# Chunk states of an attention kernel: k turned by 32x32 blocks on VectorE and through memory, in place of TensorE's transposes

## The reference, cut to what matters

```python
k = _apply_rope((hidden_states @ Wk.T).reshape(B, L, KVH, D), cos, sin)
scores = jnp.einsum('bhnid,bhnjd->bhnij', qc, kc)
k_dec = kc * jnp.exp(Glast - G)[..., None]
cstates = jnp.einsum('bhnjd,bhnje->bhnde', k_dec, xc)
_, prev = lax.scan(step, init, (chunk_decay, cstates))   # state = state * dec + cs
y_inter = jnp.einsum('bhnid,bhnde->bhnie', qc * jnp.exp(G)[..., None], prev)
```

## Time and profile before

| | us |
|---|---|
| median of 3 runs | 1811.12 |
| lowest, highest | 1809.66, 1811.59 |
| the profiled execution | 1809.74 |
| its span, first to last instruction | 1807.9 |
| PE, DVE, ACT, POOL busy | 1769.7, 1242.7, 665.1, 710.9 |

### The profile page before, as it was taken

One profiled execution on the slowest core, in us unless ns is written; L12 is line 12 of the kernel. 1 busy time (PEld: TensorE's weight loads), 2 busy tenths in 40 slices (PEclk: granted clock), 3 DMA queues, 4 the chain that ended last, 5 costly groups with the idle time before them and its releaser, 6 DMA issues.

```text
span 1807.9 us, 27508 instructions
## 1 busy us (share of the span) xinstructions
PE 1769.7 (98%) x8728; PEld 1456.6 (81%) x8728; DVE 1242.7 (69%) x2321; ACT 665.1 (37%) x2151; POOL 710.9 (39%) x757
## 2 busy tenths in 40 slices
PE   7999999999999999999999999999979999999998
PEld 5787888888888888888888888888858888888886
DVE  5235888888889888889888888988865333333332
ACT  3433444344344434444434434443543111212121
POOL 2223555456545545555555554655401101010101
PEclk9999999999999999999999999999989999999999
DMA  5333333423323332333342333333563232232321
GB/s 187 88 105 93 111 91 109 117 85 115 117 82 110 122 90 78 117 107 96 102 117 88 112 117 88 109 91 111 187 221 100 78 97 88 87 97 77 104 71 47
DMA packets 145953, 190.30 MB, mean 105 GB/s; under 512 B 9105, under 2 KB 79761, under 8 KB 145809
## 3 DMA queue, kind: packets, MB, share of 16 engines
q1 hardware_dynamic: 145808, 188.58, 34.0%
HBM read 141.89 MB, written 46.66 MB: 104 GB/s over the span
## 4 chain that ended last, share of the span: by engine, by line
PE 88%; DMA 1%; DVE 1%; ACT 0%; issue 0%; SPq 0%; POOL 0%; ACTq 0%; POOLq 0%; DVEq 0%
PE p_proj L85 29%; PE p_kept L85 14%; PE p_tok L1365 10%; PE p_kept L1365 8%; PE p_y L811 6%; PE p_score L85 5%; PE p_y L810 5%; PE p_cst L796 5%; PE p_qa L85 3%; PE p_f L1557 2%; PE p_f L1568 1%; PE p_tok L779 1%; DMA raw_shared<-in_wo_t 1%; DMA out_dram<-q 0%; DMA w_raw<-z_scratch 0%; PE p_xt L1537 0%
## 5 line engine op out<-in xcount | busy, mean ns | idle before, releaser
L114 POOL TENSOR_TENSOR q<-raw_wo_early 128x512 f32<-128x512 f32 x128 | 164.7, 1287 | 270.3 <-DVE raw_wo_early L106 270.3
L85 PE MATMUL p_proj<-shared,wq_hi 128*128 128x512 f32 x744 | 270.8, 425 | 0.0
L1077 ACT ACTIVATE square<-p_y 128x128 f32<-128x128 f32 x512 | 134.8, 277 | 260.5 <-PE p_y L811 259.3
L811 PE MATMUL p_y<-v_tok,probs 128*128 128x128 f32 x1024 | 182.1, 275 | 0.0
L85 PE MATMUL p_proj<-wg_hi,shared 128*128 128x512 f32 x528 | 175.8, 414 | 0.0
L85 PEld LDWEIGHTS p_proj<-shared,wq_hi 128*128 128x128 f32 x744 | 139.7, 188 | 43.3 <-issue 14.9
L85 PE MATMUL p_kept<-wg_hi,shared 128*128 128x512 f32 x560 | 173.3, 391 | 0.0
L952 DVE SCALAR_TENSOR_TENSOR z<-p_y,srstd,gate 128x128 f32<-128x128 f32 x512 | 143.6, 342 | 38.4 <-issue 25.6
L1052 ACT ACTIVATE probs<-g_row,stab 128x128 f32<-128x128 f32 x512 | 164.3, 410 | 9.6 <-POOL g_row L1166 9.6
L1789 POOL TENSOR_TENSOR var<-mv,eps 128x1 f32<-128x1 f32 x16 | 3.1, 192 | 411.7 <-DVE mv L1639 411.7
L1184 POOL TENSOR_TENSOR srstd<-svar,mhalf 128x4 f32<-128x4 f32 x128 | 156.8, 1225 | 10.0
(11 more groups left out here) (227 smaller groups left out, 4204.6 us busy)
## 6 DMA issues: line engine op xcount, KB each, us to landing
g_row<-g_scratch SPq DMA_DIRECT2D x128, 256.0 KB, 4.3
z_scratch<-z_st SPq DMA_DIRECT2D x256, 128.0 KB
w_raw<-z_scratch SPq DMA_DIRECT2D x62, 512.0 KB, 6.5
e_row<-e_scratch SPq DMA_DIRECT2D x96, 256.0 KB, 4.0
w_raw<-in_wq_t SPq DMA_DIRECT2D x16, 512.0 KB, 7.2
w_raw<-in_wg_t SPq DMA_DIRECT2D x16, 512.0 KB, 6.1
v_tok<-v_scratch SPq DMA_DIRECT2D x32, 256.0 KB, 2.9
v_scratch<-n_xin SPq DMA_DIRECT2D x22, 256.0 KB, 2.3
```

The source lines that it names most:

```text
L85: mm = pe.matmul(out, lhs[a], rhs[e], start=(i == 0 and j == 0), stop=(i == len(pairs) - 1 and j == 2))
L114: pool.tensor_tensor(out, keep["rope_a"][:, s, :], keep["rope_b"][:, s, :], ALU.add).then_inc(keep["roped"], 1)
L811: mm = pe.matmul(p_y[c % 2][:, h, :], probs[:, c % 2, h, :], v_tok[:, b % 2, c, :], start=(c == 0), stop=True)
L1077: s = act.activation(square[:, h, :], p_y[c % 2][:, h, :], ACT.Square, scale=2.0 / float(np.sqrt(D)), accum_out=ssum[:, c, h:h + 1])
```

## The change

For the steps after the first, DVE turns the next step's k in 32x32 blocks into a new tile k_blocks (within each block rows and columns have changed places, but the blocks themselves stand where they stood). SP stores the four bands of 32 partitions so that each block lands at its turned place in a scratch in memory, in runs of 32 numbers (128 bytes), and then loads the scratch into k_tok with positions on the partitions. k of the very first step is turned by PE as before. In `chunk_state` PE waits for that load instead of ACT's copy. k_tok is one tile, overwritten in each step after make_state 2. The transposes of PE and the copies of ACT go from the 31 steps n = 0 to 30.

```diff
SP, new functions:
+            def store_k(n):
+                sp.wait_ge(k_blocks_set, n)
+                for a in range(P // BL):
+                    sp.dma_start(k_dram.rearrange("c (b j) d -> j (c b) d", j=BL)[:, :, a * BL:(a + 1) * BL],
+                                 k_blocks[a * BL:(a + 1) * BL].rearrange("j c b i -> j (c b) i")).then_inc(k_out, 16)
+            def load_k_tok(n):
+                sp.wait_ge(k_out, 16 * (P // BL) * n)
+                sp.dma_start(k_tok[:, :, :], k_dram.rearrange("c t d -> t c d")).then_inc(k_tok_in, 16)
SP, in step, after the e_row load and before store_z and the bulk loads of the same chunk:
+                    if ahead(n):
+                        if c == 2:
+                            store_k(n + 1)
+                        elif c == 3:
+                            load_k_tok(n + 1)
PE, chunk_state:
                 if c == 0:
-                    pe.wait_ge(tok_saved, n + 1)
+                    if has_last(n):
+                        pe.wait_ge(k_tok_in, 16 * n)
+                    else:
+                        pe.wait_ge(tok_saved, 1)
PE, step:
                 gates(g, b, n, 3)
-                k_turn(n + 1, b + 1)
                 mix(g, b, n, 3)
DVE, new function:
+            def turn_k(n, b):
+                dve.wait_ge(roped, ROPED * n + 1)
+                wait_ge(dve, k_out, 16 * (P // BL) * (n - 1))
+                dve.transpose(k_blocks[:, :, :, :], k[:, b % 2, 0:(NC - 1) * C].rearrange("p (c b i) -> p c b i", c=NC - 1, i=BL)
+                              ).then_inc(k_blocks_set, 1)
DVE, step:
                 make_state(n, b, 1)
+                turn_k(n + 1, b + 1)
                 make_gate(g, b, n, 1)
ACT, step:
-                    save_k(n + 1)
build:
+                "k_dram": nc.dram_tensor("k_scratch", [NC - 1, P, D], F32).ap(),
```

More of the change, by code:

```diff
@@ L520, in attention_stage @@
         q.append(sb("q1", [P, HG, L]))
-        k_tok = sb("k_tok", [P, NC, D])
+        k_tok, k_blocks = sb("k_tok", [P, NC - 1, D]), sb("k_blocks", [P, NC - 1, TB, BL])
+        k_dram = keep["k_dram"]
         stab = sb("stab", [P, 2, NC, TAB, HG])
@@ L564, in attention_stage @@
         masked_set, xw_set = sem("masked_set"), sem("xw_set")
+        k_blocks_set, k_out, k_tok_in = sem("k_blocks_set"), sem("k_out"), sem("k_tok_in")
         q_hi_set, q_lo_set, k_hi_set, k_lo_set = sem("q_hi_set"), sem("q_lo_set"), sem("k_hi_set"), sem("k_lo_set")
@@ L773, in next_unit, with first_k_turn @@
                 project(pe, keep, w, w0, (b + 1) % B, bank(n, b, at)).then_inc(unit_done, 1)
-            def k_turn(n, b):
-                pe.wait_ge(roped, ROPED * n + 1)
-                wait_ge(pe, tok_saved, n)
+            def first_k_turn():
+                pe.wait_ge(roped, 1)
                 for c in range(NC - 1):
-                    t = pe.transpose(p_tok[:, c, :], k[:, b % 2, c * C:(c + 1) * C], ident[:, :])
+                    t = pe.transpose(p_tok[:, c, :], k[:, 0, c * C:(c + 1) * C], ident[:, :])
                 t.then_inc(tok_done, 1)
@@ L814, in first @@
             def first():
-                k_turn(0, 0)
+                first_k_turn()
             def straight(first, step):
@@ L824, in first_heads @@
             def first_heads(n, s, j, some):
-                if s == 0:
-                    pe.wait_ge(tok_saved, n + 1)
-                else:
+                if s:
                     taken(n - 1, GATE_UNIT[3])
@@ L1079, in squares, with save_first_k @@
                 s.then_inc(squares_set, 1)
-            def save_k(n):
-                act.wait_ge(tok_done, n + 1)
-                wait_ge(act, cst_done, 3 * n)
+            def save_first_k():
+                act.wait_ge(tok_done, 1)
                 act.activation(k_tok[:, 0:NC - 1, :], p_tok[:, 0:NC - 1, :], ACT.Copy).then_inc(tok_saved, 1)
@@ L1087, in first @@
                 k_high(0, 0)
-                save_k(0)
+                save_first_k()
                 q_high(0, 0, 0)
```

## The result

The changed kernel takes 1857.69 us in the median of six runs (1856.63 to 1859.31), the kernel before 1810.59 us (1809.1 to 1811.59): 1.0262 times as long, with a 95% interval of 1.0249 to 1.0275. That is 47 us more, where 1824 us, 13 more, was forecast. The profiled execution has a span of 1855.2 us.

The account below looks back on a forecast made before the run. The prediction took TensorE, busy 98% of the span, as the bound. Its terms, -10.2 us for transposes and +22.8 us for new waits, gave +12.6 us: 1824 us, range 1808 to 1843 for 8 in 10.

Parts of the forecast that it names:

- The turns off PE: At each step's end on PE: 31 triples of k transposes go, 0.33 us each, 10.2 us saved.
- VectorE: On DVE: the block transpose takes 0.53 to 0.56 us, hidden in plain steps, about 0.55 us later at b = 0.
- The places: At chunk_state: PE waits only in nine steps after bulk loads; plain steps are in time by 0.8 us.
- I do not add it: In SP's queue: four k stores' issue time, 2.86 us or less, left out beside packets of 1.6 us (1.3 to 2.7).
- The nine waits: At chunk_state after bulk loads: seven waits of 2.2 us and two of 3.7, 22.8 us in all.
- The plain steps in the loop: At chunk_state: k lands at 850.5, PE wants it at 851.26, in time by 0.8 us, so no wait.
- rival 4: On PE: half clock behind each of nine new waits loses 1.6 us each, 1838 us; chance 0.05.
- Rival 3: On the DMA engines: k store packets cost 0.043 us each, plain steps are late too, 1884 us; chance 0.09.
- Rivals 1 and 2: At chunk_state: k in time everywhere, 1800.9 us, chance 0.13; or 1.1 us late in nine steps, 1811 us, chance 0.13.

Follow-up runs that it names:

- The one wide store: The changed kernel with one k store for all 128 partitions in 1536-byte runs, instead of four in 128-byte runs: 1821.65 us.
- the kernel with both moves: The changed kernel with the k stores moved to chunk 1 and k's load right behind e_row's in chunk 2: 1801.75 us.

## Why the prediction was wrong, point by point

- **The turns off PE:** right. 10.2 us forecast, 31 x 0.35 = 10.8 found; a step without a wait takes 36.23 us, forecast 36.25; L798 has three matmuls left.
- **VectorE:** right in the size (0.57 us each x31, forecast 0.53 to 0.56) and in what hides it (the turn alone costs nothing). Missed: the lateness at the loop's jump, up to 1.0 us more, which isn't in the trace of before, where no late transfers stand there.
- **The places:** right. The nine steps named are the nine large waits; plain steps outside the loop are in time by 0.33 to 0.75 us, forecast 0.8.
- **The step that failed first, "I do not add it".** SP's issue time for the four stores was taken as lying beside the packets. The packets were cheap, at the lower bound. In a stretch of the changed kernel with almost nothing else (296.8 to 297.4 us):

```profile
DMA packets 473, 0.13 MB, mean 218 GB/s; under 512 B 435, under 2 KB 435, under 8 KB 473
...
q1 hardware_dynamic: 473, 0.13, 90.5%
```

  0.905 x 0.6 x 16 - 38 x 0.086 = 5.4 us for 435 small ones, 12.5 ns each; the packets' own records give 12.9 ns over all 48,000. That is 1.24 us for an engine. But S, the delay of all that follows, was 2.4 us in step 20 (Wq's second half landed 13.87 us after e_row's issue, before 11.45), since SP issues four stores in 2.1 us ahead of z. Bounds of 1.3 to 2.7 held it; the value taken, 1.6, was read from the packets alone. The one wide store, with packets of the same time and three issues fewer, says which of the two counts.
- **The nine waits:** 22.8 us forecast, 32.9 measured. For step 20 the forecast was 2.2 and 4.06 came: 0.8 for S (2.4 for 1.6), 0.85 for VectorE (e_row later by 1.4, not 0.55), 0.17 for the load's own time (0.87 for 0.7). They sum to 4.06. Before step 30 it was the other way, 2.46 for 3.7: there is no loop's jump, and Wo's second piece landed 14.05 us after e_row's issue, not the forecast's 1.6 us over the 13.6 of before.
- **The plain steps in the loop:** forecast in time; eleven steps waited 6.8 us. The margin was read in one plain step, and 0.8 us didn't cover what S and the loop took of it: SP needs 2.85 us for four z stores in the loop and 2.28 outside, and in step 11 the four k stores took SP 3.25 us in place of 1.9. With the stores moved ahead these waits are gone.
- **The largest term was put at nothing: the clock, rival 4.** The sum has no half clock behind the waits, and eight of the nine had it: 15.4 of the 34 us that are missing. Without them the time would have been some 1842 us, inside the range of 1808 to 1843. The reason given, "the waits forecast are shorter than that pause", was drawn from one pause and does not hold: at 3.2 to 4.2 us every wait had it, at 1.88 to 2.70 us 10 of 18 did, so even the forecast's waits of 2.2 us were no safe ground. It put 1.6 us on each, the rows show 1.5 to 1.7, or 2.7 where the low clock lasted 6.8 us. It was given 0.05 as a case of its own, when it was in truth tied to the size of the waits: half a microsecond to one more in each of them, and all of it falls due.
- **Rival 3**, small writes dear: false (12.9 ns). The rule of the Trainium skill that was set beside it, DMA: Bandwidth & Descriptors, Specifications (below 512 bytes a read-modify-write), shows no cost of its own here: the 512 packets of 128 bytes that the kernel before has, all among the loads of its first 10 us, took 13 ns each, as did the 48,000 of the changed one, nearly all stores, and the medians for 128, 512, 1024, 1536 and 2048 bytes (13, 27, 46, 65 and 84 ns) lie on one line. Short runs do cost more for each byte: the same 192 KB took a DMA engine 1.24 us as 128-byte runs and 0.52 to 0.60 as 1536-byte runs. **Rivals 1 and 2**, in time or half as late: false here, true of the kernel with both moves (1801.75, rival 1's figure was 1800.9) and of the one with the stores moved (1808.75).

In sum, 1823.7 + 7.2 for S in nine steps (9 x 0.8) + 2.9 for VectorE and the rest in them + 6.8 for small waits + 15.4 for the clock + 4.0 in the steps with waits - 0.6 for the turns - 1.0 outside the steps = 1858.4; the kernel before was 0.5 us faster in the result's runs than in those of the forecast, which gives 1857.9 for 1857.69.

## What to carry over

A transfer that an engine waits for is timed by all that its queue issues ahead of it. Count the issues (here 0.5 us each on SP) as well as the bytes, and add the two unless a row shows them side by side; put the transfer that is waited for ahead of the bulk. Where a forecast has TensorE stand idle for two microseconds or more, price the half clock behind it as a part of the same wait: here it came behind 29 of the 35 such waits. And a change that reads as a loss of 2.6% may be a gain of 0.5% in another order: test the place before giving up the idea.

## What the runs showed of the hardware that was not expected

- SP took some 0.5 us for a store whether it had 384 packets of 128 bytes or 32 of 1536 (2.1 and 1.9 us to get four of them out of the way).
- A bulk load of 1 MB right behind k_tok's load did not hold it up: 6.6 to 7.2 us from issue to landing with it, 5.7 to 7.3 in the changed kernel's steps that have no bulk; ahead of it, it cost 2.4 us in step 20.
- At the jump of a loop VectorE stands idle 1.7 to 2.1 us when SP's transfers have ended by then, and up to 5 us when they run late into it. Only the first is in a trace of a kernel that has none there. In all 65 cases its first operation starts 2 us after a packet of 8192 bytes on the instruction queue.
- How closely the half clock goes with the waits: 21 of 21 waits of 2.74 us or more, none of 39 of 0.4 to 1.83 us, each time for 3.4 or 6.8 us.
- A DMA packet's own time grew evenly with its size: medians of 13, 27, 46, 65 and 84 ns for 128, 512, 1024, 1536 and 2048 bytes, about 8 ns and 1 ns more for every 27 bytes (worked out from these five).
